# A state-space layer and a mixture of experts on one core: two maxima over partitions moved to TensorE, one weight split and group 0's pieces put later

## The chip, the cores and the metric

The kernel runs on one core of a Trainium2 chip. The metric is the device time of one launch in microseconds, and lower is better. Three runs of the kernel before took 423.21, 425.07 and 425.16 us; the median is 425.07 us.

## The reference

The input x has 2 sequences of 2048 tokens with 256 features, float32. The first half of the layer is a scan:

```
xB     = x @ B.T                                   # 256 -> 128 states
state  = tanh(state @ A.T + xB[t])                 # 2048 steps, both sequences
y      = states @ C.T + D * x + x
x1     = layernorm(x + layernorm(y) * gamma + beta)
```

The second half is a mixture of 8 experts and one shared expert, width 128, two experts for each token:

```
scores = sigmoid(x1 @ router.T);  choice = scores + correction_bias
comb   = the better half of the experts by its two best, then the two best of it, scores normed to sum 1
routed = sum over e of comb[e] * ((silu(x1 @ Wg[e]) * (x1 @ Wu[e])) @ Wd[e])
out    = layernorm(x1 + routed + shared(x1))
```

## The kernel before, in words

**Layout.** Partition p holds 32 consecutive tokens, so the 4096 tokens are 32 tiles of one token for each partition. `xres` and `xskip` hold x and x times (D+1) (later the output); `xT` holds x turned. Tiles are worked on in groups of four (`T4`), so there are G = 8 groups, each with nine experts (`E1`, 0 is the shared one).

**The scan** is made parallel over partitions: each of the 128 partitions scans its own 32 tokens from a guessed state. A first pass takes four warm-up steps and 32 steps (s = 0 to 35) and ends with a start state for each partition (`seed`). The second pass takes 32 steps (i = 0 to 31) and writes `states`. Each step is a product with `AT` on TensorE (L298) and a tanh on ScalarE (L512), each waiting for the other, and behind it TensorE issues the four products with `BT` for the next step (L292). In the first pass the transposes of x (L280) go between the steps until s = 27. At the end VectorE compares the seeds with the last states (`met_diff`, L801), takes the greatest difference per partition (L805), GpSimd takes the maximum over partitions (L951), and VectorE compares it with a bound (L808, `met`). All engines wait for `met_known`, load the value and would branch to an exact scan and a second making of group 0 (`again`) if the bound were missed. With this input it isn't missed.

**float32 as two float16 numbers.** Weights and activations go through TensorE as a scaled high part and a remainder, three products for one. The scale of each of five weights (0 `wg`, 1 `wu`, 2 router, 3 `wd`, 4 `C`) is a power of two from its greatest magnitude. VectorE takes it per partition (`greatest`, L620, into `wmax`), GpSimd over partitions (L934, between its seventh and eighth `xskip`), `scales` (L626 to L641) makes the factors, and `split(i)` (L647 the high part, L649 the remainder) makes the two parts. The order is splits 0, 1, 3, 2 in front of everything else, and split 4 in piece 4.

**Pieces of group 0.** What comes before the experts of a group is cut into pieces that are named by the expert's step at which they run for the next group. For group 0 they run in the second pass. TensorE has pieces 0 and 1 (products of `states` with `CT`, L333, two halves each), 4 and 5 (transposes of x2, L348) and 6 (logits, L359). `PE_AT` says behind which scan step each half comes. VectorE has y1, its statistics and its scaling (L690, L675, L680, L699), z1 (L706), x2 (L715) and the remainder of the turned x2 (L721); ScalarE has the high part (L494, pieces 5 and 6) and the tanh of the logits (L502, piece 7), at the steps in `ACT_AT`. GpSimd makes the reciprocal roots (L942, L944). Piece (1, half 0) on TensorE waits for VectorE's first y1, since both use one PSUM bank. Then VectorE chooses and weighs the experts (L740 to L786, `comb`). GpSimd adds `beta` to `xres` (L926, eight additions, each of four tiles): six after all its `xskip` (L918), one after each of the two roots of group 0.

**Early products.** From step `UP_FROM` = 26, behind the wait for all five splits, TensorE issues two of the 24 `wg` and `wu` products of experts 0 and 1 of group 0 at each step (`early_up`, L371), and the rest behind the scan.

**The groups.** `turn_comb` turns `comb` (L433), ScalarE copies it (L571), and SyncE writes it to HBM and reads it back as eight tiles, one for each expert, spread over all partitions (L236, L241). Per expert: TensorE's `up` (L371, twelve products), ScalarE's silu (L554), VectorE's two products (L824 for expert 0; L827 and, with the row of `comb`, L831), ScalarE's high part (L565), GpSimd's remainder (`low`, L961), TensorE's `down` with `wd` (L439, twelve products). The pieces of the next group go between. In group 0 VectorE makes piece 1 of group 1 ahead of expert 1, and piece 2 behind expert 2.

Each engine works through its queue in order, and a wait holds up all that stands behind it. These lines set the places:

```
        PE_AT = {1: (0, 0), 2: (0, 1), 4: (1, 0), 5: (1, 1), 16: (4, 0), 17: (4, 1), 20: (5, 0), 21: (5, 1),
                 24: (6, 0), 25: (6, 1)}
        ACT_AT = {18: 5, 22: 6, 26: 7}
        UP_FROM = 26
```

Of the kernel before, what the change touches and what calls it, by code (L numbers as in the profile page):

```python
# [11 lines left out]
RMAX = bass.bass_isa.ReduceOp.max  # L12
# [8 lines left out]
def ssm_moe_kernel(nc, x, A, B, C, D, gamma, beta, router_weight, correction_bias,  # L21
# [18 lines left out]
    with ExitStack() as ctx:  # L40
# [15 lines left out]
        met_row = sb("met_row", [P, 2])  # L56
        met = sb("met", [P, 1], I32)
# [25 lines left out]
        wmax_all = sb("wmax_all", [P, 5])  # L83
# [56 lines left out]
        wmax_part, wmax_known, wstep, weights_ready = sem("wmax_part"), sem("wmax_known"), sem("wstep"), sem("weights_ready")  # L140
        w_high = [sem(f"w_high{i}") for i in range(5)]

        def ahead_sems(prefix):
# [38 lines left out]
        PE_AT = {1: (0, 0), 2: (0, 1), 4: (1, 0), 5: (1, 1), 16: (4, 0), 17: (4, 1), 20: (5, 0), 21: (5, 1),  # L182
                 24: (6, 0), 25: (6, 1)}
        ACT_AT = {18: 5, 22: 6, 26: 7}
        UP_FROM = 26
# [68 lines left out]
        def _(pe):  # L254
# [55 lines left out]
            for s in range(WARM + L):  # L310
                scan_step(s, tiles, seeds if s in (0, WARM) else run_state[:, (s - 1) % 2, :])
                if s < HALVES:
                    turn_x(FIRST + s // 2, s % 2)
                if s == WARM:
                    turn_Cr()

# [75 lines left out]
            for i in range(L):  # L392
# [5 lines left out]
                if i == UP_FROM:  # L398
                    pe.wait_ge(weights_ready, 5)
# [7 lines left out]

            pe.wait_ge(met_known, 1)
# [60 lines left out]
            turn_comb(0)  # L469
            group(0, 0, first=True)  # L470
# [130 lines left out]
        def _(dve):  # L601
            nc.vector.memset(seed[:, :, :], 0.0).then_inc(seed_clear, 1)
            nc.vector.memset(fb_state[:, :, :], 0.0).then_inc(seed_clear, 1)
            dve.wait_ge(AB_turned, 1)
# [18 lines left out]
            def scales():  # L623

                dve.wait_ge(wmax_known, 1)
                nc.vector.tensor_scalar(wpow[:, :], wmax_all[:, :], 2.0 ** -60, None, ALU.max).then_inc(wstep, 1)  # L626
# [42 lines left out]
            for i in (0, 1, 3, 2):  # L669
# [121 lines left out]
            dve.wait_ge(weights_ready, 4)  # L791
            for e in range(E1):
                piece(e, 0, 0, main)
                if e == 4:
                    split(4)
            choose(0, main)
# [11 lines left out]
            nc.vector.tensor_scalar(met[:, :], met_row[:, 1:2], MET, None, ALU.is_le).then_inc(met_known, 1)  # L808
# [87 lines left out]
        def _(pool):  # L896
# [32 lines left out]
            for n in range(L // T4):  # L929
                skip(n)  # L930
                if n == 6:

                    pool.wait_ge(wmax_part, 5)
                    nc.gpsimd.partition_all_reduce(wmax_all[:, :], wmax[:, :], P, RMAX).then_inc(wmax_known, 1)  # L934
# [15 lines left out]
            pool.wait_ge(met_part, 1)  # L950
            nc.gpsimd.partition_all_reduce(met_row[:, 1:2], met_row[:, 0:1], P, RMAX).then_inc(met_all, 1)  # L951
# [58 lines left out]
```

## Time and profile before

| | |
|---|---|
| median of 3 runs | 425.07 us (423.21 to 425.16) |
| span of the profiled execution | 423.6 us |
| its own time | not listed; the page gives its span alone |
| TensorE busy (weight loads) | 378.8 us, 89% (254.6 us, 60%) |
| VectorE busy | 323.5 us, 76% |
| ScalarE busy | 138.0 us, 33% |
| GpSimd busy | 163.7 us, 39% |
| mean granted clock of TensorE | 0.965 |

Times inside an execution are microseconds from its first instruction. In the rows PE is TensorE, PEld its weight loads, DVE VectorE, ACT ScalarE, POOL GpSimd and SP SyncE; a q behind an engine's name is its queue of instructions that count as no work. L12 is line 12 of the kernel before. A float32 product of 128 columns appears as two instructions. Idle time stands in brackets with what ended it; "issue" means that the profile shows nothing that was waited for. Busy shares are averages over a scan and eight groups that have different limits, so the stretches are read one by one. Span and device time of an execution needn't be equal.

### The profile page before, as it was taken

The numbers are of one execution on the slowest core, as the hardware profiler recorded it, in microseconds if no ns is written. First come the engines' busy times: TensorE is split into PE (matmuls) and PEld (weight loads), VectorE is DVE, ScalarE is ACT, GpSimd is POOL, SyncE is SP. The second block draws the span as 40 slices with busy tenths as digits, with TensorE's granted clock in tenths as the row PEclk, the third lists the DMA queues.
The fourth block names the chain that finished last, engine by engine and source line by source line (L and its number), as shares of the span: only waits on it lengthen the run. The fifth ranks groups of instructions, "written<-read, shape, count | busy, mean of one in ns | idle before, by whom it ended". The sixth has DMA issues, their size and how long they took to land.

```text
span 423.6 us, 7485 instructions
## 1 busy us (share of the span) xinstructions
PE 378.8 (89%) x2583; PEld 254.6 (60%) x2583; DVE 323.5 (76%) x740; ACT 138.0 (33%) x280; POOL 163.7 (39%) x151
## 2 busy tenths in 40 slices
PE   6899529596999998999899999999998999899992
PEld 5899428582566665666556556655565565565561
DVE  2343998445587699979978997999699969984464
ACT  2454102132233423242433244233432342333330
POOL 1870697300442334235423542344244234514242
PEclk9999958699899999999999999999999999999997
DMA  7980000003800460153018211901260145016311
GB/s 187 315 300 2 0 0 2 0 2 63 140 2 0 86 117 2 52 123 79 7 47 152 49 52 34 158 8 50 68 132 0 50 109 93 0 53 141 59 52 50
DMA packets 15901, 29.95 MB, mean 71 GB/s; under 512 B 1720, under 2 KB 4288, under 8 KB 15872
## 3 DMA queue, kind: packets, MB, share of 16 engines
q1 hardware_dynamic: 15872, 29.58, 29.9%
q8 instruction: 17, 0.28, 0.3%
q14 instruction: 12, 0.10, 0.1%
HBM read 25.24 MB, written 4.33 MB: 70 GB/s over the span
## 4 chain that ended last, share of the span: by engine, by line
issue 28%; PE 22%; POOL 18%; DVE 18%; DMA 5%; SPq 5%; ACT 2%; POOLq 1%; DVEq 0%; ACTq 0%
PE bank L371 11%; POOL h L961 9%; PE bank L439 4%; POOL xres L926 4%; DVE st L675 3%; SPq L205 3%; POOL rstd L944 3%; DVE wu L706 3%; DVE xT L827 3%; DMA xT<-comb_dram 2%; PE bank L292 2%; DVE xT L831 2%; DVE wg L715 2%; DMA xres<-in_L_attn_x_dram 2%; PE bank L298 1%
## 5 line engine op out<-in xcount | busy, mean ns | idle before, releaser
L961 POOL TENSOR_TENSOR h<-xT,h 128x512 f16<-128x512 f32 x72 | 86.2, 1198 | 185.8 <-ACT h L565 177.0
L439 PE MATMUL bank<-wd,h 128*128 128x256 f16 x864 | 106.9, 274 | 5.6 <-POOL h L961 4.9
L371 PE MATMUL bank<-x2T,wg 128*128 128x512 f16 x432 | 105.3, 379 | 0.0
L371 PE MATMUL bank<-x2T,wu 128*128 128x512 f16 x432 | 105.3, 379 | 0.0
L439 PEld LDWEIGHTS bank<-wd,h 128*128 128x128 f16 x864 | 84.4, 98 | 30.5 <-POOL h L961 5.7
L565 ACT ACTIVATE h<-xT 128x512 f16<-128x512 f32 x72 | 45.3, 630 | 131.7 <-DVE xT L831 128.2
L371 PEld LDWEIGHTS bank<-x2T,wu 128*128 128x128 f16 x432 | 42.3, 98 | 50.3
L827 DVE SCALAR_TENSOR_TENSOR xT<-bank,u_un,xT 128x512 f32<-128x512 f32 x64 | 47.6, 744 | 23.1 <-ACT xT L554 22.2
L554 ACT ACTIVATE xT<-bank,g_un 128x512 f32<-128x512 f32 x72 | 49.2, 683 | 43.2 <-PE bank L371 40.4
L371 PEld LDWEIGHTS bank<-x2T,wg 128*128 128x128 f16 x432 | 41.8, 98 | 35.6 <-issue 0.3
L831 DVE TENSOR_TENSOR xT<-xT 128x512 f32<-128x512 f32 x64 | 44.3, 692 | 8.4 <-DMA xT<-comb_dram 6.5
L292 PE MATMUL bank<-xT,BT 128*128 128x128 f32 x272 | 44.7, 290 | 0.0
L292 PEld LDWEIGHTS bank<-xT,BT 128*128 128x128 f32 x272 | 38.9, 206 | 0.1
L944 POOL TENSOR_TENSOR rstd<-rstd,neghalf 128x4 f32<-128x4 f32 (+1 forms) x25 | 25.6, 1025 | 2.0
L918 POOL TENSOR_TENSOR xskip<-xres,D_bc 128x1024 f32<-128x1024 f32 x8 | 20.5, 2586 | 10.3 <-issue 7.3
L675 DVE BATCH_NORM_STATS2 st<-wu 128x6 f32<-128x256 f32 x64 | 23.3, 416 | 0.8
L512 ACT ACTIVATE states<-bank 128x128 f32<-128x128 f32 x32 | 8.9, 278 | 42.2 <-PE bank L298 42.2
L706 DVE SCALAR_TENSOR_TENSOR wu<-wu,rstd,xres 128x256 f32<-128x256 f32 x32 | 21.7, 742 | 1.0 <-POOL rstd L944 1.0
L926 POOL TENSOR_TENSOR xres<-xres,beta_bc 128x1024 f32<-128x1024 f32 x8 | 22.3, 2815 | 0.0
L348 PE MATMUL bank<-ident,wg 128*128 128x128 f32 x64 | 11.2, 294 | 12.4 <-DVE wg L715 7.7
L715 DVE TENSOR_SCALAR wg<-wu,mv,rstd 128x256 f32<-128x256 f32 x32 | 19.7, 679 | 1.7 <-POOL rstd L944 1.4
L333 PE MATMUL bank<-CT,states 128*128 128x256 f32 x16 | 6.4, 516 | 13.0 <-DVE wu L690 13.0
(114 smaller groups left out, 356.8 us busy)
## 6 DMA issues: line engine op xcount, KB each, us to landing
xT<-comb_dram SPq DMA_DIRECT2D x64, 256.0 KB, 7.5
xres<-in_L_attn_x_dram SPq DMA_DIRECT2D x7, 512.0 KB, 5.9
out_dram<-xskip SPq DMA_DIRECT2D x7, 512.0 KB, 2.7
wd<-in_L_ffn_w_down_dram SPq DMA_DIRECT2D x1, 1024.0 KB, 7.0
xres<-in_L_attn_x_dram SPq DMA_DIRECT2D x2, 256.0 KB, 3.4
out_dram<-xskip SPq DMA_DIRECT2D x2, 256.0 KB, 2.0
B_sb<-in_L_attn_B_dram SPq DMA_DIRECT2D x1, 128.0 KB, 2.2
C_sb<-in_L_attn_C_dram SPq DMA_DIRECT2D x1, 128.0 KB
```

What stands on the lines that cost most here:

```text
L292: pe.matmul(ps_scan[s % 2][:, 0:P], BT[:, k, :], xT[:, k, tile, :], start=(k == 0), stop=False)
L371: last = pe.matmul(ps[:, :], w[:, pw, e, m // 3, :], x2T[:, par, px, m // 3, :], start=(m == 0), stop=(m == NUP // 2 - 1))
L439: return pe.matmul(ps_y[t // 2][:, (t % 2) * DM:(t % 2 + 1) * DM], h16[:, e % 3, ph, t * P:(t + 1) * P], wd16[:, pw, e, :], start=start, s ...
L554: nc.scalar.activation(sg[:, b, :], ps_g[b][:, :], ACT.Silu, scale=g_un[:, 0:1]).then_inc(silu_done, 1)
L565: nc.scalar.activation(h16[:, e % 3, 0, :], h[:, b, :], ACT.Copy).then_inc(h_high, 1)
L675: nc.vector.bn_stats(st[:, k, t, :], src(t)).then_inc(st_sem, 1)
L706: nc.vector.scalar_tensor_tensor(y1[:, t, :], y1[:, t, :], rstd[:, 0, 1, t:t + 1], xres[:, g * T4 + t, :], ALU.mult, ALU.add).then_inc(sem ...
L827: nc.vector.scalar_tensor_tensor(gu[:, b, :], ps_u[b][:, :], u_un[:, 0:1], sg[:, b, :], ALU.mult, ALU.mult).then_inc(gu_done, 1)
L831: nc.vector.tensor_tensor(h[:, b, :], comb_all[:, e - 1, :], gu[:, b, :], ALU.mult).then_inc(h_done, 1)
L926: nc.gpsimd.tensor_tensor(xres[:, c * T4:(c + 1) * T4, :], xres[:, c * T4:(c + 1) * T4, :], beta_bc[:, :].unsqueeze(1).to_broadcast([P, T4 ...
L944: nc.gpsimd.tensor_tensor(rstd[:, k, 1, t0:t1], rstd[:, k, 0, t0:t1], neghalf[:, t0:t1], ALU.pow).then_inc(ready, 1)
L961: nc.gpsimd.tensor_tensor(h16[:, e % 3, 1, :], h[:, b, :], h16[:, e % 3, 0, :], ALU.subtract).then_inc(h_low, 1)
```

## The change

The two maxima over partitions leave GpSimd. The five weight maxima are turned by TensorE (behind step s = 30 of the first pass), reduced by VectorE, spread on a diagonal and brought to all partitions by a product with ones (behind s = 32). The greatest difference of the seeds is turned by TensorE behind its early products and reduced by VectorE on one partition. The split of `wd` goes from in front of y1 to behind piece 6 on VectorE, so TensorE waits for three splits at `UP_FROM` and for all five ahead of group 0. In the second pass piece 1 on TensorE goes from steps 4 and 5 to 10 and 11, pieces 4, 5 and 6 from 16 to 25 to 26 to 31, ScalarE's from 18, 22 and 26 to 27, 29 and 31, and `UP_FROM` is 31.

```diff
--- before.py
+++ after.py
@@ -9,7 +9,6 @@
 F16 = mybir.dt.float16
 I32 = mybir.dt.int32
 AX_X = mybir.AxisListType.X
-RMAX = bass.bass_isa.ReduceOp.max
 P = 128
 
 LN_EPS = 1e-5
@@ -53,8 +52,9 @@
         seed = sb("seed", [P, NB, NCH])
         fb_state = sb("fb_state", [P, 2, NB])
         met_diff = sb("met_diff", [P, NB, NCH - 1])
-        met_row = sb("met_row", [P, 2])
-        met = sb("met", [P, 1], I32)
+        met_row = sb("met_row", [P, 1])
+        met_top = sb("met_top", [1, 1])
+        met = sb("met", [1, 1], I32)
         act_warm = sb("act_warm", [P, 1])
 
         ident = sb("ident", [P, P])
@@ -80,7 +80,9 @@
         wu16 = sb("wu16", [P, 2, E1, KT, I], F16)
         wd16 = sb("wd16", [P, 2, E1, DM], F16)
         wmax = sb("wmax", [P, 5])
-        wmax_all = sb("wmax_all", [P, 5])
+        wmax_row = sb("wmax_row", [5, 1])
+        wmax_diag = sb("wmax_diag", [5, 5])
+        ones = sb("ones", [5, P])
         wpow = sb("wpow", [P, 5])
         wscale = sb("wscale", [P, 5])
         g_un = sb("g_un", [P, 1])
@@ -137,7 +139,8 @@
         met_step, met_part, met_all, met_known = sem("met_step"), sem("met_part"), sem("met_all"), sem("met_known")
         fb_mm, fb_tanh, fb_kept = sem("fb_mm"), sem("fb_tanh"), sem("fb_kept")
         skip_done, res_done = sem("skip_done"), sem("res_done")
-        wmax_part, wmax_known, wstep, weights_ready = sem("wmax_part"), sem("wmax_known"), sem("wstep"), sem("weights_ready")
+        wmax_part, wmax_turned, wmax_step, wmax_known = sem("wmax_part"), sem("wmax_turned"), sem("wmax_step"), sem("wmax_known")
+        wstep, weights_ready = sem("wstep"), sem("weights_ready")
         w_high = [sem(f"w_high{i}") for i in range(5)]
 
         def ahead_sems(prefix):
@@ -179,10 +182,10 @@
         HALVES = 2 * (len(pairs) - FIRST)
 
 
-        PE_AT = {1: (0, 0), 2: (0, 1), 4: (1, 0), 5: (1, 1), 16: (4, 0), 17: (4, 1), 20: (5, 0), 21: (5, 1),
-                 24: (6, 0), 25: (6, 1)}
-        ACT_AT = {18: 5, 22: 6, 26: 7}
-        UP_FROM = 26
+        PE_AT = {1: (0, 0), 2: (0, 1), 10: (1, 0), 11: (1, 1), 26: (4, 0), 27: (4, 1), 28: (5, 0), 29: (5, 1),
+                 30: (6, 0), 31: (6, 1)}
+        ACT_AT = {27: 5, 29: 6, 31: 7}
+        UP_FROM = 31
         WHOLE = 2
         NUP = 2 * 3 * KT
 
@@ -313,6 +316,14 @@
                     turn_x(FIRST + s // 2, s % 2)
                 if s == WARM:
                     turn_Cr()
+                if s == WARM + 26:
+
+                    pe.wait_ge(wmax_part, 5)
+                    pe.transpose(ps_mats[0][0:5, 0:P], wmax[:, :], ident[:, :]).then_inc(wmax_turned, 1)
+                if s == WARM + 28:
+
+                    pe.wait_ge(wmax_step, 3)
+                    pe.matmul(ps_mats[0][:, P:P + 5], ones[:, :], wmax_diag[:, :], start=True, stop=True).then_inc(wmax_known, 1)
 
             def piece(e, g, par, sems, halves=(0, 1)):
 
@@ -396,7 +407,7 @@
                     e, half = PE_AT[i]
                     piece(e, 0, 0, main, halves=(half,))
                 if i == UP_FROM:
-                    pe.wait_ge(weights_ready, 5)
+                    pe.wait_ge(weights_ready, 3)
                 if i >= UP_FROM:
                     for n in (n_up, n_up + 1):
                         early_up(n)
@@ -405,6 +416,8 @@
                 early_up(n)
 
 
+            pe.wait_ge(met_part, 1)
+            pe.transpose(ps_misc[0:1, 0:P], met_row[:, 0:1], ident[:, :]).then_inc(met_all, 1)
             pe.wait_ge(met_known, 1)
             runs_met = pe.value_load(met[0:1, 0:1], min_val=0, max_val=1)
             with pe.If(runs_met == 0):
@@ -467,6 +480,7 @@
                         piece(e, g + 1, 1 - par, main)
 
             turn_comb(0)
+            pe.wait_ge(weights_ready, 5)
             group(0, 0, first=True)
             group(1, 1)
             with pe.Fori(1, G // 2 - 1) as two:
@@ -601,6 +615,7 @@
         def _(dve):
             nc.vector.memset(seed[:, :, :], 0.0).then_inc(seed_clear, 1)
             nc.vector.memset(fb_state[:, :, :], 0.0).then_inc(seed_clear, 1)
+            nc.vector.memset(ones[:, :], 1.0).then_inc(wmax_step, 1)
             dve.wait_ge(AB_turned, 1)
             nc.vector.tensor_copy(AT[:, :], ps_mats[0][:, 0:P])
             nc.vector.tensor_copy(BT[:, :, :].rearrange("p k n -> p (k n)"), ps_mats[0][:, P:(KT + 1) * P]).then_inc(AB_done, 1)
@@ -622,8 +637,12 @@
 
             def scales():
 
+                dve.wait_ge(wmax_turned, 1)
+                nc.vector.tensor_reduce(wmax_row[:, :], ps_mats[0][0:5, 0:P], AX_X, ALU.max).then_inc(wmax_step, 1)
+                dve.wait_ge(wmax_step, 2)
+                nc.vector.tensor_scalar(wmax_diag[:, :], ident[0:5, 0:5], wmax_row[:, 0:1], None, ALU.mult).then_inc(wmax_step, 1)
                 dve.wait_ge(wmax_known, 1)
-                nc.vector.tensor_scalar(wpow[:, :], wmax_all[:, :], 2.0 ** -60, None, ALU.max).then_inc(wstep, 1)
+                nc.vector.tensor_scalar(wpow[:, :], ps_mats[0][:, P:P + 5], 2.0 ** -60, None, ALU.max).then_inc(wstep, 1)
                 dve.wait_ge(wstep, 1)
                 nc.vector.tensor_scalar(wpow[:, :].bitcast(I32), wpow[:, :].bitcast(I32), 0x7F800000, None,
                                         ALU.bitwise_and).then_inc(wstep, 1)
@@ -666,7 +685,7 @@
                 dve.wait_ge(w_in[min(i, 2)], 16 * 2)
                 greatest(i)
             scales()
-            for i in (0, 1, 3, 2):
+            for i in (0, 1, 2):
                 split(i)
 
             def stats(k, g, src, st_sem, mv_sem, t0, t1):
@@ -788,11 +807,13 @@
 
 
             dve.wait_ge(res_done, 2)
-            dve.wait_ge(weights_ready, 4)
+            dve.wait_ge(weights_ready, 3)
             for e in range(E1):
                 piece(e, 0, 0, main)
                 if e == 4:
                     split(4)
+                elif e == 6:
+                    split(3)
             choose(0, main)
             weigh(0, main)
 
@@ -805,7 +826,9 @@
             nc.vector.tensor_reduce(met_row[:, 0:1], met_diff[:, :, :].rearrange("p b c -> p (b c)"), AX_X, ALU.max,
                                     apply_absolute_value=True).then_inc(met_part, 1)
             dve.wait_ge(met_all, 1)
-            nc.vector.tensor_scalar(met[:, :], met_row[:, 1:2], MET, None, ALU.is_le).then_inc(met_known, 1)
+            nc.vector.tensor_reduce(met_top[:, :], ps_misc[0:1, 0:P], AX_X, ALU.max).then_inc(met_step, 1)
+            dve.wait_ge(met_step, 2)
+            nc.vector.tensor_scalar(met[:, :], met_top[:, :], MET, None, ALU.is_le).then_inc(met_known, 1)
             dve.wait_ge(met_known, 1)
             runs_met = dve.value_load(met[0:1, 0:1], min_val=0, max_val=1)
             with dve.If(runs_met == 0):
@@ -928,10 +951,6 @@
 
             for n in range(L // T4):
                 skip(n)
-                if n == 6:
-
-                    pool.wait_ge(wmax_part, 5)
-                    nc.gpsimd.partition_all_reduce(wmax_all[:, :], wmax[:, :], P, RMAX).then_inc(wmax_known, 1)
             pool.wait_ge(vecs_in, 16 * NVEC)
             for n in range(L // T4 - 2):
                 residual(n)
@@ -947,8 +966,6 @@
             residual(L // T4 - 2)
             rsqrt(1, 0, main["mv2_done"], rstd_step, main["rstd2_ready"], 1)
             residual(L // T4 - 1)
-            pool.wait_ge(met_part, 1)
-            nc.gpsimd.partition_all_reduce(met_row[:, 1:2], met_row[:, 0:1], P, RMAX).then_inc(met_all, 1)
             pool.wait_ge(met_known, 1)
             runs_met = pool.value_load(met[0:1, 0:1], min_val=0, max_val=1)
             with pool.If(runs_met == 0):
```

## Rows read from the trace of the kernel before

**Rows 1.** Busy time by stretch, 140 to 180: us, then PE, PEld, DVE, ACT, POOL busy

```profile
140.00:180.00 40.00, 38.69 (x266) 23.90 (x264) 35.69 (x88) 13.88 (x23) 14.71 (x15) 1.00 0.35 67
```

**Rows 2.** GpSimd in order of time: start us, length us, then idle before and releaser

```profile
29.82 2.36 POOL L918 TENSOR_TENSOR xskip<-xres,D_bc 128x1024 f32<-128x1024 f32 x1 [2.32 <-DMA xres<-in_L_attn_x_dram]
37.84 0.39 POOL L934 PARTITION_ALL_REDUCE wmax_all<-wmax  x1 [5.67 <-issue]
45.55 4.20 POOL L918 TENSOR_TENSOR xskip<-xres,D_bc 128x1024 f32<-128x1024 f32 x1 [7.32 <-issue]
```

**Rows 3.** VectorE in order of time, from the scales to the comparison

```profile
38.27 0.17 DVE L626 TENSOR_SCALAR wpow<-wmax_all 128x5 f32<-128x5 f32 x1 [7.24 <-POOL wmax_all L934]
...
39.49 1.42 DVE L647 TENSOR_SCALAR wg<-wg,wscale 128x2304 f16<-128x2304 f32 x1
...
47.47 3.50 DVE L647 TENSOR_SCALAR wd<-wd,wscale 128x2304 f16<-128x2304 f32 x1
...
55.50 2.31 DVE L647 TENSOR_SCALAR rw<-rwT,wscale 128x16 f16<-128x16 f32 x1
...
60.20 0.69 DVE L690 TENSOR_TENSOR wu<-bank,xskip 128x512 f32<-128x512 f32 x1
...
65.07 0.68 DVE L690 TENSOR_TENSOR wu<-bank,xskip 128x512 f32<-128x512 f32 x1
...
86.51 0.69 DVE L721 SCALAR_TENSOR_TENSOR x2T<-bank,x2T 128x512 f16<-128x512 f32 x1 [3.31 <-ACT x2T L494]
90.02 0.18 DVE L740 TENSOR_SCALAR score<-th 128x32 f32<-128x32 f32 x1 [2.82 <-ACT th L502]
...
94.77 0.19 DVE L786 TENSOR_TENSOR comb<-kept,total 128x32 f32<-128x32 f32 x1
95.41 0.29 DVE L801 TENSOR_TENSOR met_diff<-states,seed 128x126 f32<-128x126 f32 x1 [0.44 <-ACT states L512]
```

**Rows 4.** TensorE in order of time, from the first pass to group 0

```profile
37.95 0.49 PE L298 MATMUL bank<-run_state,AT 128*128 128x128 f32 x2
...
43.08 0.49 PE L298 MATMUL bank<-seed,AT 128*128 128x128 f32 x2
...
60.95 1.22 PE L333 MATMUL bank<-CT,states 128*128 128x256 f32 x2 [13.02 <-DVE wu L690]
...
64.09 0.63 PE L298 MATMUL bank<-states,AT 128*128 128x128 f32 x2
...
65.37 0.63 PE L298 MATMUL bank<-states,AT 128*128 128x128 f32 x2
...
73.24 0.49 PE L298 MATMUL bank<-states,AT 128*128 128x128 f32 x2
...
78.85 0.69 PE L348 MATMUL bank<-ident,wg 128*128 128x128 f32 x2 [4.67 <-DVE wg L715]
...
96.55 1.46 PE L371 MATMUL bank<-x2T,wu 128*128 128x512 f16 x6
98.05 0.60 PE L433 MATMUL bank<-ident,comb 128*8 128x128 f32 x4
...
106.81 2.32 PE L439 MATMUL bank<-wd,h 128*128 128x256 f16 x12 [4.71 <-POOL h L961]
```

**Rows 5.** Instructions of line L961: length ns min/median/max, first and last start us

```profile
L961 POOLq MODIFY_POOL_CONFIG  x2: 11/11/11, 97.8 to 98.1; - x2
```

**Rows 6.** All engines in order of time, from the comparison into group 0

```profile
97.69 0.69 ACT L554 ACTIVATE xT<-bank,g_un 128x512 f32<-128x512 f32 x1 [2.38 <-DVE met L808]
...
105.06 0.69 DVE L831 TENSOR_TENSOR xT<-xT 128x512 f32<-128x512 f32 x1 [2.16 <-DMA xT<-comb_dram]
...
110.87 0.69 DVE L690 TENSOR_TENSOR wu<-bank,xskip 128x512 f32<-128x512 f32 x1 [2.38 <-PE bank L333]
...
112.67 0.91 DVE L699 SCALAR_TENSOR_TENSOR wu<-wu,mv,gamma_bc 128x256 f32<-128x256 f32 x2
...
115.58 2.57 DVE L706 SCALAR_TENSOR_TENSOR wu<-wu,rstd,xres 128x256 f32<-128x256 f32 x4
```

## The prediction

> **What bounds the kernel now.** I read the busy table by stretches first. From 140 us on the groups are TensorE's (38.7 of 40 us busy), and the change touches nothing inside them [rows 1]. So the gain or loss lies before about 120 us, and I went through the engines' timelines there in order of time.
>
> GpSimd first. Its maximum over partitions takes 0.39 us, but 5.67 us of idle stand before it and 7.32 us behind it, and VectorE waits 7.24 us for the result [rows 2, 3]. TensorE next: it stands still 13.0 us before the second product with `CT` (released by the y1 of L690) and again before the transposes of x2 at 78.85, and for 4.7 us before the first product with `wd` at 106.81, released by GpSimd [rows 4]. VectorE explains the first: its splits run one after another from 39.49, `wd` alone takes from 47.47 to 55.50, and y1 comes at 60.20 [rows 3]. The last is GpSimd again: its first subtraction of group 0 starts 8.8 us late, and its queue shows two configuration instructions at 97.8 to 98.1 us, 7.2 us before that start at 105.36, the same distance as behind the first maximum [rows 2, 5]. I read the gaps as GpSimd changing its code for each maximum and back.
>
> **The two maxima.** Removed: two instructions of 0.4 us, the 5.67 and 7.32 us around the first, and the 7.2 us behind the second. (The one before the second lies in a wait of GpSimd and costs nothing now.)
>
> Added for the first: a transpose in TensorE's queue at step s=30 of the first pass, a reduction and a 5x5 multiply on VectorE, a product with ones at s=32. TensorE's position is what decides. The second pass starts at 43.08 and a step takes 0.855 us ((43.08-37.95)/6), so s=30 is at 37.95 and s=32 at 39.7 [rows 4]. The five maxima are ready at 31.0 (7.24 before 38.27), 6.9 us before that, so this handover makes nothing earlier: transpose about 39.0, reduction about 39.5, product about 40.7, where GpSimd delivered at 38.2 [rows 3]. The scales start later than now by 2.5 us at least.
>
> What gains is GpSimd's own queue. It finished its seventh `xskip` at 32.18 and would do the eighth and the six additions to `xres` at once, each 2.36 us when nothing is in its way (the same shape) [rows 2]: 34.5 plus 6 times 2.35 is 48.6 us, without VectorE in between. Now they run beside the splits, and both engines pay: `xskip` at 45.55 took 4.20 us, a VectorE scaling of 16 columns took 2.31 [rows 2, 3]. In the timeline each holds the other off for a whole instruction. The Trainium skill, page "SBUF — State Buffer", section "SBUF: two separate sides", calls this an exclusive lock held for a full instruction, taken on VectorE by two-port forms or by two SBUF inputs; the trace agrees for `xskip` and for the 16 columns.
>
> Whether operations of one or five columns are held off too, no row shows. If none is, the scales end at 42.0 and the splits of `wg` and `wu` (7.98 us together, from 39.49 to 47.47) [rows 3] meet three additions of 2.35: about 56.5, and 0.4 for `rw`. If all are, the 5x5 multiply waits to 41.7, which also keeps TensorE standing at s=32 for 1.1 us, three more wait to 44.1, 46.5 and 48.9, and then the splits run free: 49.3 + 8.0 + 0.4 = 57.7. I take 57.8, as the 16 columns are nearest. y1 comes 2.4 us earlier than at 60.20. The scan delayed by 1.1 us is hidden: it reaches its wait for y1 at about 53 to 54.
>
> **The moved pieces.** The second half of the first piece now waits at i=10 instead of i=4. TensorE stops there at about 53.5 and goes on at 58.5: 5 us of stall where there are 13.0, but six steps further along. The next step's product behind the second `CT` product came 3.1 us after the restart (60.95 to 64.09) [rows 4]; again so, the second y1 starts at 61.9 (now 65.07). From there to the first half of x2 (78.85) VectorE took 13.8 us [rows 3, 4]; GpSimd no longer ends an addition first, which was 0.5 us: half of x2 at 75.2. The two last additions still run beside it, and their cost is inside the 13.8.
>
> The scan meets this well. From 64.09 ten steps took 9.15 us, to 73.24 [rows 4], the half clock at their start included (1.28 us for a step at 64.09, 0.855 later). The new i=12 is at 61.7, i=22 at 70.9, i=26 at 74.3, its transposes at 75.1. Stall: nearly none. Had they stayed at i=16, the wait would be back. Then, one piece a step, copy and remainder on ScalarE and VectorE between: the second `x2T` remainder ends at about 80.8 (now 86.51 + 0.69) [rows 3] and the scan at about 81.5.
>
> **The split of `wd`.** Removed before y1: 8.03 us (47.47 to 55.50) [rows 3]. Added after the `x2T` remainder: half of 7.98, 4.0 us, no GpSimd work beside it. It ends at 84.8; `th` is there at about 82, so it delays the routing by 2.7 us. The routing takes 4.94 us (90.02 to the end of `comb` at 94.96): `comb` at 89.9 [rows 3]. TensorE loses its ten early products inside the scan; 24 come after it. Six took 1.46 us [rows 4], so they need under 6 us, to 87, while VectorE is not done. Cover is VectorE's routing; without it they would be on the path.
>
> **The second maximum.** From the end of `comb` to ScalarE's first silu 2.73 us pass [rows 3, 6]. Of these 0.44 went to waiting for the last tanh [rows 3], gone now; I estimate that transpose and reduction on one row take some 0.4 us more than the maximum on GpSimd. Kept at 2.7: 92.6 us, and all engines wait for that. The bounds are 0.2 less, and 1.0 more if TensorE, idle from 87 us, does this at the half clock. `turn_comb` starts at 92.6 instead of 98.05: **5.4 us**.
>
> **Group 0.** GpSimd is ready when its first `h` is. But the rows of `comb` still come by DMA about 7 us after `turn_comb` (98.05 to 105.06) [rows 4, 6]. I count on in the old times. From 105.06 VectorE is at work, with ScalarE between, to 108.5, where it stood 2.38 us for TensorE [rows 6]; now the second `CT` product is there, so its y1 work of 2.7 us (110.87 to 113.58) runs to 111.2, the next pair of products to 112.7, and the four z1 instructions start there, not at 115.58: 2.9 us sooner [rows 6]. TensorE by itself would be 5.5 us ahead (5.4 + the half clock at 106.81 [rows 4]), so it waits some 2.5 us for x2 of group 1, and the gain is **2.9 us**. What is late next is VectorE's chain, not TensorE.
>
> Sum: 5.4 + 2.9 = 8.3 us, span 423.6 - 8.3 = 415.3. The profiled execution's own time isn't listed; the median of the runs, 425.07, is 1.4 above its span, so 416.7 us.
>
> A rule against the change: the first maximum on GpSimd costs 0.39 us of work [rows 2], less than the four instructions replacing it. The Trainium skill, "VectorE: DVE Perf Modes", section "Rules for kernel authors", says to reduce along partitions on GpSimd. By the rule the old form stays and the time is 425.07; by the rows the gaps around it are what costs, not the work.
>
> **Rivals.** (a) Group 0 is TensorE's alone: VectorE fits its y1 work in, and the full 5.5 us come through: 5.4 + 5.5 = 10.9, 414.2 us. For it: 2.38 us of VectorE idle at 110.87. Against: the order in its queue. (b) The late scales eat the gain before y1: VectorE is held off at every small instruction, or the product at s=32 comes late, and y1 stays at 60.2. Then 2.4 us less: 419.1. (c) The gap at 98 us is not a change of code but comes from the branch on `met`; then GpSimd's 8.8 us stay, and only the shift of `met`, 5.1 us, remains: 420.0. For it: a branch does stand there. Against: the first maximum has the same 7.3 us and no branch. The Trainium skill, "GPSIMD Engine Reference", section "Instruction dispatch", puts the first call of freshly loaded code at about 6 us; it speaks of the load alone, and the 5.67 us agree. By it the way back is not priced, which is case (c). (d) Slower: TensorE stays at the half clock from the restart at i=10 through the scan, and on into group 0. Steps then take 1.28 us, i=26 comes 6 us late, `turn_comb` at about 99.6, 1.6 later than now. Against that stand the 2.9 of group 0, and half of every microsecond at the half clock there; over 6.8 us of it make the kernel measurably slower, 13.6 make 1.6 - 2.9 + 6.8 = 5.5, 430.6 us. Against: of the ten steps from 64.09, in 9.15 us, only the first two were slow [rows 4]. (e) Smaller losses together, about no change: 424.
>
> **How the numbers follow.** Forecast 0.58, (a) 0.12, (b) 0.12, (c) 0.09, (d) 0.04, (e) 0.05. The forecast's own spread is 1.5 us to each side (the small columns, 1.0; the clock at `met`, 0.8). Range 413.2 to 420.4: it takes in (a), (b) and (c) and leaves out (d), (e) and errors beyond the steps. A measurement here tells 0.5% (2.1 us) from nothing. Faster 0.91, same 0.05, slower 0.04.
>
> **What would show it.** No configuration instructions and no gaps of 5 to 7 us in GpSimd's timeline; its additions begun by 35 us; y1 at 56.8 to 57.8; the wait at i=10 near 5 us, that at x2 under 1; `turn_comb` near 92.6; the first `wd` product released without a late GpSimd, and a new wait of about 2.5 us before the transposes of x2 in group 0. A `turn_comb` later than 95, or a TensorE stall at i=26 of 3 us, would make it wrong.

## The result, and the profile after

The kernel after takes 413.52 us (median of 4, 412.04 to 414.61) against 424.62 us for the kernel before in the same comparison: ratio 0.9746, 95% interval 0.9716 to 0.9776, 11.1 us faster. Measured once more beside later experiments it took 413.50 us, ratio 0.9745 (0.972 to 0.9769). The profiled execution took 412.55 us.

The page of the kernel after, in parts (the slices are 10.3 us wide):

```profile
span 410.8 us, 7488 instructions
...
PE 378.9 (92%) x2587; PEld 252.9 (62%) x2587; DVE 320.2 (78%) x744; ACT 138.0 (34%) x280; POOL 157.2 (38%) x149
...
PEclk9999989979999999999999999999999999999997
```

The span is 12.8 us shorter, though TensorE's busy time is the same. Of these 12.8, some 1.6 us are no gain of the change: the last of the five weight maxima per partition starts at 26.88 us here and at 28.48 in the profile before, and in the ten profiles of the experiments it lies between 26.2 and 27.8; it waits for the load of `wd`. How long the kernel before waits for its input in its other executions no profile shows; the device times, all executions together, give 11.1.

GpSimd in order of time:

```profile
28.19 4.69 POOL L941 TENSOR_TENSOR xskip<-xres,D_bc 128x1024 f32<-128x1024 f32 x2 [2.29 <-DMA xres<-in_L_attn_x_dram]
32.83 13.93 POOL L949 TENSOR_TENSOR xres<-xres,beta_bc 128x1024 f32<-128x1024 f32 x6
60.35 0.20 POOL L961 TENSOR_TENSOR rstd<-mv,eps 128x4 f32<-128x4 f32 x1 [13.60 <-DVE mv L699]
...
90.92 1.16 POOL L978 TENSOR_TENSOR h<-xT,h 128x512 f16<-128x512 f32 x1 [19.82 <-ACT h L579]
```

Against [rows 2] the two gaps of 5.67 and 7.32 us are gone, and the six additions to `xres` (L949) start at 32.83 and end at 46.76, not at 67.37. The first `h` remainder follows its `h` at 90.92, without the 8.8 us; its line has no configuration instruction as in [rows 5] any more.

VectorE in order of time; of its rows those that answer to [rows 3], and two of the new ones:

```profile
37.41 0.28 DVE L641 TENSOR_REDUCE wmax_row<-bank 5x1 f32<-5x128 f32 x1 [7.97 <-PE bank L322]
37.72 2.12 DVE L643 TENSOR_SCALAR wmax_diag<-ident,wmax_row 5x5 f32<-5x5 f32 x1
...
42.19 2.28 DVE L651 TENSOR_SCALAR wscale<-wpow 128x5 int32<-128x5 int32 x1
44.38 0.14 DVE L653 TENSOR_SCALAR g_un<-wpow 128x1 f32<-128x1 f32 x1
...
45.11 2.87 DVE L666 TENSOR_SCALAR wg<-wg,wscale 128x2304 f16<-128x2304 f32 x1
...
55.13 0.69 DVE L709 TENSOR_TENSOR wu<-bank,xskip 128x512 f32<-128x512 f32 x1
...
58.51 0.69 DVE L709 TENSOR_TENSOR wu<-bank,xskip 128x512 f32<-128x512 f32 x1 [0.71 <-PE bank L344]
...
76.36 0.69 DVE L740 SCALAR_TENSOR_TENSOR x2T<-bank,x2T 128x512 f16<-128x512 f32 x1 [2.05 <-ACT x2T L508]
76.96 1.41 DVE L666 TENSOR_SCALAR wd<-wd,wscale 128x2304 f16<-128x2304 f32 x1
...
80.94 0.17 DVE L759 TENSOR_SCALAR score<-th 128x32 f32<-128x32 f32 x1
...
85.68 0.19 DVE L805 TENSOR_TENSOR comb<-kept,total 128x32 f32<-128x32 f32 x1
...
87.19 0.14 DVE L831 TENSOR_SCALAR met<-met_top 1x1 int32<-1x1 f32 x1
...
102.86 2.56 DVE L725 SCALAR_TENSOR_TENSOR wu<-wu,rstd,xres 128x256 f32<-128x256 f32 x4
```

y1 comes at 55.13 (60.20 before), `comb` at 85.68 (94.77), `met` at 87.19 (96.57); each of these differences holds the 1.6 us of the input. The 5x5 multiply took 2.12 us and the making of `wscale` on five columns 2.28, while the operation on one column at 44.38 took 0.14. GpSimd's additions at those times, from two narrower windows of the timeline:

```profile
42.09 2.35 POOL L949 TENSOR_TENSOR xres<-xres,beta_bc 128x1024 f32<-128x1024 f32 x1
```
```profile
44.40 2.36 POOL L949 TENSOR_TENSOR xres<-xres,beta_bc 128x1024 f32<-128x1024 f32 x1
```

The five-column operation at 42.19 starts just after the addition at 42.09 has started and ends with it, at 44.47 (the addition at 44.44). The six one-column operations lie beside the next addition (44.40 to 46.76) and aren't held; the split at 45.11 is: it takes 2.87 us where 1.42 is its own.

TensorE in order of time:

```profile
36.33 0.49 PE L301 MATMUL bank<-run_state,AT 128*128 128x128 f32 x2
...
39.90 0.38 PE L326 MATMUL bank<-wmax_diag,ones 5*128 5x5 f32 x2 [0.92 <-DVE wmax_diag L643]
...
43.62 0.49 PE L301 MATMUL bank<-states,AT 128*128 128x128 f32 x2
...
55.87 0.70 PE L344 MATMUL bank<-CT,states 128*128 128x256 f32 x2 [3.12 <-DVE wu L709]
...
58.27 0.64 PE L301 MATMUL bank<-states,AT 128*128 128x128 f32 x2
...
71.63 0.44 PE L359 MATMUL bank<-ident,wg 128*128 128x128 f32 x2
...
77.72 0.45 PE L370 MATMUL bank<-rw,x2T 128*128 128x8 f16 x12
...
81.91 1.46 PE L382 MATMUL bank<-x2T,wu 128*128 128x512 f16 x6
86.57 0.27 PE L420 MATMUL bank<-ident,met_row 128*1 128x128 f32 x1 [3.20 <-DVE met_row L826]
88.69 1.02 PE L446 MATMUL bank<-ident,comb 128*8 128x128 f32 x4 [1.85 <-issue]
...
95.30 1.47 PE L452 MATMUL bank<-wd,h 128*128 128x256 f16 x12
...
109.49 0.66 PE L359 MATMUL bank<-ident,wg 128*128 128x128 f32 x4
```

Against [rows 4]: the stop for y1 is 3.12 us instead of 13.02, the first transposes of x2 (71.63) come without a wait, and a wait of 3.20 us for the met difference is new. The last step's logits end at 78.2, the early products at 83.4. `turn_comb` starts 9.4 us sooner, at 88.69, and the four z1 instructions of group 1 (102.86) 12.7 us sooner than in [rows 6].

### The profile page after: what moved, and what is told of

Same layout as the page of the kernel before. It is cut to its first block, busy times and chain, and to the rows that moved or that the text cites. A ratio compares the mean times of both kernels' runs of the same rounds, so it can differ in the third digit from the quotient of the medians.

```text
span 410.8 us, 7488 instructions
## 1 busy us (share of the span) xinstructions
PE 378.9 (92%) x2587; PEld 252.9 (62%) x2587; DVE 320.2 (78%) x744; ACT 138.0 (34%) x280; POOL 157.2 (38%) x149
## 4 chain that ended last, share of the span: by engine, by line
issue 27%; DVE 24%; PE 22%; POOL 12%; DMA 7%; SPq 5%; ACT 2%; POOLq 1%; DVEq 0%; ACTq 0%
PE bank L382 9%; POOL h L978 9%; PE bank L452 4%; DMA xT<-comb_dram 3%; DVE st L694 3%; PE bank L295 3%; DVE xT L850 3%; SPq L208 3%; DVE xT L854 3%; POOL rstd L963 2%; PE bank L301 2%; DMA xres<-in_L_attn_x_dram 2%; DVE wu L725 2%; DMA comb_dram<-combT 1%; DVE wg L734 1%
## 5 line engine op out<-in xcount | busy, mean ns | idle before, releaser
L295 PE MATMUL bank<-xT,BT 128*128 128x128 f32 x272 | 43.6, 285 | 0.0
L295 PEld LDWEIGHTS bank<-xT,BT 128*128 128x128 f32 x272 | 37.5, 200 | 0.1
L961 POOL TENSOR_TENSOR rstd<-mv,eps 128x4 f32<-128x4 f32 (+1 forms) x25 | 6.9, 274 | 35.7 <-DVE mv L699 35.7
L941 POOL TENSOR_TENSOR xskip<-xres,D_bc 128x1024 f32<-128x1024 f32 x8 | 18.7, 2364 | 3.9 <-DMA xres<-in_L_attn_x_dram 3.8
L949 POOL TENSOR_TENSOR xres<-xres,beta_bc 128x1024 f32<-128x1024 f32 x8 | 18.6, 2354 | 0.0
```

What stands on the lines that cost most here:

```text
L295: pe.matmul(ps_scan[s % 2][:, 0:P], BT[:, k, :], xT[:, k, tile, :], start=(k == 0), stop=False)
```

## The experiments

All ratios are to the kernel before, with 95% intervals. "Changed" is the kernel after.

| run | time us | ratio |
|---|---|---|
| changed again | 413.50 | 0.9745 (0.9720 to 0.9769) |
| first maximum on GpSimd | 417.30 | 0.9824 (0.9795 to 0.9853) |
| second maximum on GpSimd | 414.73 | 0.9773 (0.9736 to 0.9810) |
| pieces as before | 418.47 | 0.9841 (0.9811 to 0.9871) |
| `wd` in front | 415.97 | 0.9794 (0.9767 to 0.9820) |
| maxima alone | 422.06 | 0.9942 (0.9917 to 0.9966) |
| order alone | 418.43 | 0.9859 (0.9835 to 0.9882) |
| first maximum turned sooner | 412.59 | 0.9715 (0.9689 to 0.9740) |
| and additions between | 409.35 | 0.9662 (0.9637 to 0.9686) |
| and retimed | 406.23 | 0.9575 (0.9549 to 0.9600) |

**The changed kernel again.**

> The changed kernel itself, unedited, beside the runs of this call. 413.5 us, ratio 0.9746 within its interval; it gives the base for the differences of a few us here.

It is the base for the differences below.

**One part undone at a time: the first maximum.**

```diff
-                if s == WARM + 26:
...
-                if s == WARM + 28:
...
+                if n == 6:
+                    pool.wait_ge(wmax_part, 5)
+                    nc.gpsimd.partition_all_reduce(wmax_all[:, :], wmax[:, :], P, RMAX).then_inc(wmax_known, 1)
```

> The changed kernel with the first maximum (five weight maxima) back on GpSimd. Theory A (what I forecast: the first maximum gains only through GpSimd's freed queue, and the additions to xres still fill it until about 60 us): the scales end sooner, near 38 us, y1 comes near 46 us instead of 55.1, but GpSimd starts its eight-us-late additions at about 46 us and makes the first reciprocal root only behind six of them, near 60 to 61 us, where the changed kernel has it at 60.6. So the time is that of the changed kernel within 1.5 us: 412 to 415. Rival B (the first maximum on GpSimd costs what it shows, gaps of 5.7 and 7.3 us on the path): 5 us or more slower than the changed kernel, 418.5 or more.

Measured 3.8 us slower than the changed kernel; neither bound was met. GpSimd's timeline of this run, then y1 in VectorE's:

```profile
35.98 0.39 POOL L946 PARTITION_ALL_REDUCE wmax_all<-wmax  x1 [5.50 <-issue]
43.84 4.05 POOL L931 TENSOR_TENSOR xskip<-xres,D_bc 128x1024 f32<-128x1024 f32 x1 [7.47 <-issue]
47.86 14.46 POOL L939 TENSOR_TENSOR xres<-xres,beta_bc 128x1024 f32<-128x1024 f32 x6
62.27 0.39 POOL L954 TENSOR_TENSOR rstd<-mv,eps 128x4 f32<-128x4 f32 x1
```

```profile
52.55 0.69 DVE L699 TENSOR_TENSOR wu<-bank,xskip 128x512 f32<-128x512 f32 x1 [2.31 <-POOL xres L939]
```

The mechanism of theory A is there: the gaps return, the scales are ready at 36.4, the splits end at 50.2, and VectorE, which could then make y1, waits for the second addition to `xres` until 52.55; my 46 us for y1 had left out this wait, which stands in VectorE's queue (`res_done`, 2). The first root starts at 62.27, 1.9 us later than in the changed kernel (60.35), since y1's two-input operations and the additions hold each other off. x2 is then 2.1 us late (70.88 against 68.81), TensorE stops 4.69 us for it, and it goes on at the half clock, granted from 71.6 to 78.4 us. `comb` comes 3.6 us late. Where I had expected nothing, 2 us are hold-offs and 1.5 us arise between x2 and `comb`, where the two traces differ in this stop and in the half clock behind it; neither was tried by itself.

**The second maximum.**

```diff
-            pe.transpose(ps_misc[0:1, 0:P], met_row[:, 0:1], ident[:, :]).then_inc(met_all, 1)
...
+            nc.gpsimd.partition_all_reduce(met_row[:, 1:2], met_row[:, 0:1], P, RMAX).then_inc(met_all, 1)
```

> The changed kernel with the second maximum (seed difference) back on GpSimd. Theory A (GpSimd changes its code back after the maximum, 7.2 us): the two configuration instructions and a gap of 8 to 9 us return in front of the first h remainder, TensorE waits 3 to 5 us for it, and the kernel is 3.0 us slower than the changed one, about 416.5. Rival C (the gap belongs to the branch on met): it is there in the changed kernel too, and the time stays within 0.5 us of the changed one; that kernel's profile already speaks against it.

Measured 1.2 us slower than the changed kernel, not 3.0; the difference is within the two intervals, so the time alone doesn't tell it from nothing, but its trace shows a loss of that size. All engines in order of time:

```profile
95.73 0.69 DVE L851 TENSOR_TENSOR xT<-xT 128x512 f32<-128x512 f32 x1 [0.68 <-DMA xT<-comb_dram]
95.94 2.61 POOL L977 TENSOR_TENSOR h<-xT,h 128x512 f16<-128x512 f32 x2 [8.54 <-issue]
...
97.49 1.48 PE L451 MATMUL bank<-wd,h 128*128 128x256 f16 x12 [2.05 <-POOL h L977]
```

The gap of 8.54 us is back, so it goes with the maximum and not with the branch on `met`, which the changed kernel has too. But the row of `comb` arrives by DMA at 95.73, 0.2 us before GpSimd is ready: the gap is nearly covered. TensorE's stop is 2.05 us. From `turn_comb` to x2 of group 1 the kernel before takes 23.4 us (98.05 to 121.41), this run 21.5 (88.95 to 110.41) and the changed kernel 20.0. So GpSimd is 1.5 of the 3.4 us that group 0 gained. In the other 1.9, the traces differ in where TensorE's half clock lies: from 107.3 to 110.7 in the kernel before, right where TensorE starts to be the bound; from 87.1 to 93.9 here and 87.4 to 94.2 in the changed kernel, while everything waits for the row of `comb`. The run with the order alone has GpSimd's gap and the half clock at 89.1 to 95.9, and takes 21.5 us too (92.05 to 113.59). The same products stand in both traces at either clock: from the first product with `wd` to the `wg` products behind the four `CT` products 3.82 us pass in the kernel before (106.81 to 110.63, granted 0.5 from 107.3) and 2.19 in this run (97.49 to 99.68, granted 1.0). That is 1.6 of the 1.9 us. A run that moves the half clock alone wasn't made.

**The pieces.**

```diff
-        PE_AT = {1: (0, 0), 2: (0, 1), 10: (1, 0), 11: (1, 1), 26: (4, 0), 27: (4, 1), 28: (5, 0), 29: (5, 1),
-                 30: (6, 0), 31: (6, 1)}
-        ACT_AT = {27: 5, 29: 6, 31: 7}
-        UP_FROM = 31
+        PE_AT = {1: (0, 0), 2: (0, 1), 4: (1, 0), 5: (1, 1), 16: (4, 0), 17: (4, 1), 20: (5, 0), 21: (5, 1),
+                 24: (6, 0), 25: (6, 1)}
+        ACT_AT = {18: 5, 22: 6, 26: 7}
+        UP_FROM = 26
```

> The changed kernel with group 0's pieces at the steps of the kernel before (4, 5, 16 to 25, early products from 26), the split of wd still late. Theory A (the scan is not what ends last; VectorE's chain is, and TensorE only has to be there in time): TensorE waits some 8 us at i=4 for y1 and 1 to 2 us at i=16, the scan ends near 86 us, comb near 87, turn_comb near 89 to 90: 0.5 to 1.5 us slower than the changed kernel, 414 to 415. Rival D (the later places are what saves the wait of 13 us, as the stall at y1 suggests): 5 us or more slower, 418.5.

Measured 5.0 us slower than the changed kernel by the medians, 4.1 by the two ratios: theory A missed, and D's number of 5 or more was just met. TensorE's waits in this run:

```profile
56.39 1.22 PE L344 MATMUL bank<-CT,states 128*128 128x256 f32 x2 [8.24 <-DVE wu L709]
...
72.89 0.69 PE L359 MATMUL bank<-ident,wg 128*128 128x128 f32 x2 [3.27 <-DVE wg L734]
...
94.64 0.60 PE L446 MATMUL bank<-ident,comb 128*8 128x128 f32 x4 [1.82 <-issue]
```

TensorE stops 8.24 us for y1, as expected, and 3.27 us for x2, then fifteen steps are still to come. They end at 90.0, 17 us after the restart at 72.89, with the half clock from 72.0 to 78.8 us and early products inside; in the changed kernel only five steps are left behind x2, and the scan ends at 78.2. `comb` is ready at 90.7, as late as the scan. I had expected 1 to 2 us of stop at x2 and the end of the scan near 86. A second thing I had left out is the place of the new transpose: it stands behind all early products in TensorE's queue, so with the scan this late it comes at 92.55, 1.2 us after VectorE has its operand.

**The split of `wd`.**

```diff
-            for i in (0, 1, 2):
+            for i in (0, 1, 3, 2):
...
-                elif e == 6:
-                    split(3)
```

(with the waits for the splits as before).

> The changed kernel with the split of wd back in front of y1, pieces at the later steps. Theory A: y1 at 59.1 instead of 55.1 (4.0 us), the second x2T remainder near 80.4 us, no split between it and the routing, which then waits for the logits: comb 0.7 to 1.5 us later than in the changed kernel, 414 to 415. Rival E (the split in front costs its full 4 us or, with GpSimd beside it, 8 us): 417.5 or more.

2.5 us slower, between the two expectations; the intervals of the two ratios just touch. y1 is at 59.00 as counted and x2 4.6 us late (73.43); the routing starts 2.2 us late (83.15 against 80.94), since the split no longer stands before it. The stop for y1 is 7.1 us, and the half clock lasts from 54.9 to 65.1. So of the 8 us that this split took in front in the kernel before, 4 were hold-offs by GpSimd, which the freed queue ends even with the split in front, and of the other 4 us 2.5 show in the time.

**Half of the change at a time.** Maxima alone is the kernel after with the two edits above together (pieces and `wd` as before); order alone is the kernel after with both maxima on GpSimd.

> The kernel before with both maxima off GpSimd and nothing else: wd split in front, pieces at the early steps. The scan must end last here, as in the run with early pieces: y1 at 59, x2 begins at 73.4, its transposes near 76.2, 17 us of scan behind them (16.5 in the kernel before), turn_comb near 95, then 1.5 to 3.3 us in group 0. Theory S (scan and VectorE's chain bound in turn, so the parts need each other): 419 to 421. Rival M (the maxima are nearly all of the gain, order and split are details): 415.5 or less.

> The kernel before with the order alone: split of wd late, pieces at the later steps, both maxima on GpSimd. Theory S: the parts' prices in the changed kernel, 3.8 us for the first maximum and 1.2 for the second, add up: 418 to 419. Rival M (maxima are nearly all): 423 or more. If the four variants add, maxima alone and order alone together give the 11 us; if they need each other, they give less.

The maxima alone give 0.6% (2.6 us), the order alone 1.4% (6.2 us), together 11.1: the sum of the halves is 2.3 us short, so each needs the other. Theory S holds; for the maxima alone the gain was smaller than I had counted (422.1, not 419 to 421). The scan ended at 92.8 us, 2.5 us sooner than in the kernel before, and `turn_comb` came at 97.44, only 0.6 us sooner; the rest lies in group 0. The new transpose takes the difference, since it stands behind the early products, which the maximum on GpSimd ran beside. VectorE's timeline of the maxima alone has this:

```profile
95.66 0.28 DVE L827 TENSOR_REDUCE met_top<-bank 1x1 f32<-1x128 f32 x1 [2.14 <-PE bank L420]
```

In the changed kernel the early products end at 83.4, and the same wait is 0.36 us. So the second maximum on TensorE is free only with the order that ends the scan early. In the order alone TensorE's waits are these:

```profile
52.80 0.70 PE L338 MATMUL bank<-CT,states 128*128 128x256 f32 x2 [2.06 <-DVE wu L697]
...
73.19 0.69 PE L353 MATMUL bank<-ident,wg 128*128 128x128 f32 x2 [5.95 <-DVE wg L722]
...
92.05 1.01 PE L438 MATMUL bank<-ident,comb 128*8 128x128 f32 x4 [5.19 <-issue]
```

The stop for y1 is short even with both maxima on GpSimd: the late place of the piece hides it. The stop for x2 stays (5.95 us), as GpSimd's additions still lie beside y1 and in front of the first root.

**Where y1's time comes from.**

```diff
-                if s == WARM + 26:
+                if s == WARM + 20:
...
-                if s == WARM + 28:
+                if s == WARM + 22:
```

> The changed kernel with the transpose and the product for the first maximum six steps sooner (s = 24 and 26), right when the five maxima are ready. Theory L (GpSimd and VectorE hold each other off for whole instructions; the six additions and the splits together fill the time from 33 to 55 us whatever starts first): the scales start near 33 but meet six additions of 2.35 us instead of three, y1 at 54 to 56 us, time within 1 us of the changed kernel. Rival P (the position in TensorE's queue is what y1 waits for, as I priced it): y1 5 us sooner, near 50; the scan then is what x2 waits for, and the time falls by 2 us or more.

412.59 us, 0.9 less, within the intervals. GpSimd's six additions and then VectorE's timeline of this run:

```profile
33.77 18.48 POOL L949 TENSOR_TENSOR xres<-xres,beta_bc 128x1024 f32<-128x1024 f32 x6
```

```profile
35.36 0.17 DVE L645 TENSOR_SCALAR wpow<-bank 128x5 f32<-128x5 f32 x1 [1.51 <-PE bank L326]
...
39.12 2.86 DVE L666 TENSOR_SCALAR wg<-wg,wscale 128x2304 f16<-128x2304 f32 x1
42.02 4.58 DVE L668 SCALAR_TENSOR_TENSOR wg<-wg,wscale 128x2304 f16<-128x2304 f32 x1
46.53 3.51 DVE L666 TENSOR_SCALAR wu<-wu,wscale 128x2304 f16<-128x2304 f32 x1
50.08 4.59 DVE L668 SCALAR_TENSOR_TENSOR wu<-wu,wscale 128x2304 f16<-128x2304 f32 x1
...
55.18 0.69 DVE L709 TENSOR_TENSOR wu<-bank,xskip 128x512 f32<-128x512 f32 x1
```

The scales are ready 5 us sooner (35.36 against 40.31) and y1 is at 55.18, as before the edit (the input of this profile came 1.0 us later, so the edit may have given up to that). Each split half now takes the addition beside it as well: 2.86, 4.58, 3.51 and 4.59 us where 1.42 and 2.62 are their own, and the six additions take 18.5 us instead of 13.9. Rival P falls.

**The additions between.** GpSimd makes two additions, waits for the three splits, then the others.

```diff
             for n in range(L // T4 - 2):
+                if n == 2:
+                    pool.wait_ge(weights_ready, 3)
                 residual(n)
```

> The kernel of the run before (transpose and product for the first maximum six steps sooner), and GpSimd makes two of its additions to xres first and the other four only when the three front splits are done. Theory L (whole-instruction hold-offs fill the time): the splits run in their own 8 us, y1 near 47 us instead of 55.2; then the scan, which reaches its first use of y1 at i=10 near 52, and the four additions beside the y1 work bound the rest: turn_comb 2 to 4 us sooner, 409 to 411. Rival N (the additions only move, and cost the same beside the y1 work): 412 to 413, no gain.

409.35 us, 4.1 less than the changed kernel. GpSimd's additions:

```profile
33.68 4.66 POOL L949 TENSOR_TENSOR xres<-xres,beta_bc 128x1024 f32<-128x1024 f32 x2
47.57 9.67 POOL L949 TENSOR_TENSOR xres<-xres,beta_bc 128x1024 f32<-128x1024 f32 x4 [9.23 <-DVE rw L668]
```

y1 is at 47.59, 7.6 us sooner, as theory L has it. Two thirds of that are lost again: the four additions run from 47.57 to 57.2, first beside y1's scaling and then in front of the first root (57.21), and x2's scaling starts at 65.90, 2.5 us sooner than in the run before.

**Retimed.** On top of it: two of those additions go behind the first root and the second, the last two behind x2; pieces 1, 4, 5, 6 at steps 5, 6 and 24 to 29, early products from 30; the high part of `wd` behind the first `x2T` remainder; the split of `C` behind the comparison of `met`.

```diff
+        PE_AT = {1: (0, 0), 2: (0, 1), 5: (1, 0), 6: (1, 1), 24: (4, 0), 25: (4, 1), 26: (5, 0), 27: (5, 1),
+                 28: (6, 0), 29: (6, 1)}
+        ACT_AT = {25: 5, 27: 6, 29: 7}
+        UP_FROM = 30
...
+                if e == 5:
+                    split(3, (0,))
+                elif e == 6:
+                    split(3, (1,))
...
+            residual(5)
+            pool.wait_ge(main["x2_ready"], T4)
+            residual(6)
+            residual(7)
```

> The same, and the rest put where the engines are idle: two more additions only after the first root, the last two behind x2; pieces at steps 5, 6 and 24 to 29; the high part of wd while VectorE waits for the second x2T, the split of C behind the met comparison. Theory L: y1 near 47, transposes of x2 near 65, comb near 79 to 80, turn_comb near 82: 406 to 408. Rival N: TensorE's scan, at its free pace until step 24 near 65 us, doesn't let x2 be used sooner than now, and collisions move behind x2: 410 or more.

406.23 us: ratio 0.9575, 7.3 us less than the changed kernel and the fastest here. y1 at 47.34, x2's scaling at 62.67, `comb` at 80.03, `turn_comb` at 83.81 (near 82 expected). The stop for y1 is gone; the largest left is 2.0 us at the second `x2T`, where one addition holds the high part of `wd` for 2.1 us.

## Why the prediction was right, and where it was off

The forecast was 416.7 us (413.2 to 420.4), 8.3 us faster; measured 413.5, 11.1 us. The mechanism was right in its main steps, but the time lies 3.2 us from the forecast, beyond its own spread of 1.5, and inside the range only because the range took in case (a), 414.2. That case's mechanism isn't what happened, so its nearness is luck. In the profile `turn_comb` came at 88.69, not 92.6: 1.7 us of this is the earlier input, 1.0 us lies before y1, 0.9 from y1 to x2 and 0.3 behind it; group 0 adds 0.5. By its steps:

- **GpSimd's code.** Right in kind, as far as the runs show it: no configuration instructions, no gaps, and with the second maximum back the gap is back. That code is loaded in the gap is a reading of the configuration instructions. Case (c) falls.
- **The scales start later.** Right: 40.31 against 38.27, though everything else is sooner. TensorE stood 0.92 us at s=32 for the held 5x5 multiply (counted 1.1).
- **y1 at 57.8.** Measured 55.13. The additions started at 32.83, not 34.5, as the input came sooner in all profiles after: 1.7 us that are no error of the count. The term that was too large, by 1.0 us, is the hold-offs of the small operations: those on one column aren't held, so the last addition meets a split and not the small ones. My lower end for y1, 56.8, was already too late, and the stop at i=10 was 3.12 us, not near 5.
- **From y1 to x2.** The second y1 came 3.4 us behind the first, not 4.1 (3.4 us at the half clock fell on TensorE's work here, 5.4 in the kernel before); the transposes at 71.63, not 75.2. The scan met them without a stop, as said.
- **Split, routing, comparison.** The remainder of `x2T` ends 5.4 us after the transposes (counted 5.6), the split takes 4.0 (4.0), the routing 4.9 (4.94), from `comb` to `turn_comb` 2.8 (2.7). TensorE idled 3.2 us before the comparison and ran `turn_comb` at the half clock, the bound I had named.
- **Group 0.** Right: 3.4 us (counted 2.9), and what ends last is VectorE's chain. z1 at 102.86, 7.3 us behind the row of `comb` (95.52), is the 7.6 us counted (105.06 to 112.7), so case (a) is not it. Of the 3.4 us, 1.5 go with GpSimd's gap and most of the others with the half clock on the `wd` and `CT` products. The announced stop of about 2.5 us before the transposes of x2 hardly shows in the profile above (0.15 us), because the half clock until 94.2 had kept TensorE busy with the products before. It is 0.76 us in the second profile of the changed kernel and 2.0 us where `turn_comb` met the full clock, as in the retimed one:

```profile
110.43 0.66 PE L359 MATMUL bank<-ident,wg 128*128 128x128 f32 x4 [0.76 <-DVE wg L734]
```
```profile
104.36 0.66 PE L359 MATMUL bank<-ident,wg 128*128 128x128 f32 x4 [2.02 <-DVE wg L738]
```

In eight of the nine profiles without GpSimd's gap these transposes start 20.4 to 20.8 us behind `turn_comb`, whatever TensorE's clock was (the ninth, the maxima alone, has 21.4); in the kernel before it was 24.3. The 5.5 us by which TensorE would be ahead are, by [rows 4], its wait of 4.71 and about 0.8 for the half clock at 106.81; the 5.4 in the prediction's bracket is no part of them.

Case (b) fell with y1, and (d) and (e) with the time. The Trainium skill's lock rule ("SBUF — State Buffer", "SBUF: two separate sides") is borne out by the held splits (2.87 us beside an addition, 1.42 alone). The Trainium skill's rule to reduce along partitions on GpSimd ("VectorE: DVE Perf Modes", "Rules for kernel authors") doesn't give the faster kernel here: with the first maximum there it is 3.8 us slower.

What the prediction had not seen is how the parts share the gain. The maxima, where it looked for the cause, are the smaller half (2.6 us alone); the order gives 6.2 us even with the gaps in place. Nor had it seen that the second transpose comes behind the early products, since in the changed kernel nothing shows of it.

## What to carry to other kernels

A rare instruction on GpSimd can cost idle time on both sides of it, 5.5 to 7.5 us each here; look for configuration instructions in its queue before moving anything, and then ask what covers the gap. When VectorE and GpSimd work on SBUF together, count their held-off instructions as one queue: starting one of them 5 us sooner moved y1 by 1.0 us at most (55.13 and 55.18, with the input 1.0 us later), taking four additions out of the other's way moved y1 by 7.6 us. Put a dependent piece at the last step of a chain at which it is still in time, so that few steps stand behind the wait. A maximum moved to TensorE waits behind what TensorE has queued: 2.14 us with a late scan, 0.36 with an early one.

## What the runs showed of the hardware

- VectorE's operations on five float32 columns from SBUF to SBUF are held by a running GpSimd instruction (the 5x5 multiply 2.12 us against 0.26 in the run with the transpose sooner, `wscale` 2.28 against 0.17 in the kernel before); those on one column aren't (0.14 us beside an addition).
- Around the `partition_all_reduce` of the weight maxima GpSimd idled 5.5 to 5.7 us before it and 6.9 to 7.5 behind it, in each of the three profiles that have it, and a pair of configuration instructions stands at the start of each gap.
- TensorE's granted clock has two levels here, 1.0 and 0.5 (2.4 and 1.2 GHz). Half-clock stretches of very different lengths go with its stops: 3.4 us behind the stop of 3.12 us; 13.7 where it stood 13.0 us, 8.3 of them inside the stop and 5.4 on its work; none at the stop for y1 in the order alone (2.06 us). Its place mattered more than its length: ahead of the row of `comb` 6.8 us of it (changed kernel), 3.4 us (turned sooner) and none (pieces as before) leave 14.1 to 14.2 us from `turn_comb` to z1 of group 1.
